# Products of ones in front of fifteen waits of TensorE, written into the work bank that is taken next

## The reference

```
x = x + xattn0(layernorm(x), ctx, mask, ...)    # 16 heads of 32, masked softmax
x = x + ffn0(layernorm(x), packed ternary weight, scale, bias)
x = x + xattn1(layernorm(x), ctx, ...)          # 16 heads of 64, softmax, Wo
x = x + ffn1(layernorm(x), w_freq, bias)        # fft, product, inverse fft
```

## Time and profile before

| | |
|---|---|
| three runs, median (lowest to highest) | 1057.13 us (1056.42 to 1057.41) |
| the profiled execution | 1054.12 us |
| its span in the profile | 1052.3 us |
| mean granted clock of TensorE over the span | 0.952 |
| PE busy | 904.6 us (86%), 6236 matmuls |
| DVE busy | 837.3 us (80%) |
| ACT busy | 639.2 us (61%) |
| POOL busy | 576.9 us (55%) |

### The profile page before, as it was taken

The page is one execution under the profiler, slowest core; times in us unless marked ns, Lnnn a source line. Parts: engine busy times, 40 slices in busy tenths (PEclk is TensorE's granted clock), DMA queues, the critical chain, the costliest instruction groups (busy, mean ns, idle before and its releaser), DMA issues. The chain is left out here.

```text
span 1052.3 us, 17974 instructions
## 1 busy us (share of the span) xinstructions
PE 904.6 (86%) x6236; PEld 498.7 (47%) x6236; DVE 837.3 (80%) x1451; ACT 639.2 (61%) x1792; POOL 576.9 (55%) x596
## 2 busy tenths in 40 slices
PE   0698988696888989998999899989999998798598
PEld 0446764252544554544455445545554545344343
DVE  7777968489999789979978997898889978755624
ACT  2435755275786487758765976697568756615610
POOL 2404774535274569456954784677378554636303
PEclk9999989798898999999999999999999999899599
DMA  9570475857574766765694669385946655621605
GB/s 290 133 173 20 102 147 131 166 119 206 95 124 96 132 113 125 151 137 108 119 190 92 119 114 201 66 152 105 204 78 128 120 91 117 109 64 36 125 1 160
DMA packets 352906, 130.41 MB, mean 124 GB/s; under 512 B 333487, under 2 KB 342640, under 8 KB 349999
## 3 DMA queue, kind: packets, MB, share of 16 engines
q1 hardware_dynamic: 352815, 129.25, 60.1%
HBM read 33.57 MB, written 15.96 MB: 47 GB/s over the span
## 5 line engine op out<-in xcount | busy, mean ns | idle before, releaser
L878 POOL TENSOR_TENSOR pr<-pr,sm 128x616 f32<-128x616 f32 x128 | 177.5, 1387 | 230.0 <-DVE sm L1391 230.0
L1031 ACT ACTIVATE pr<-scores,bound,factor 128x77 f32<-128x77 f32 x576 | 230.1, 418 | 6.9 <-ACT bound L1025 0.4
L262 PE MATMUL wb<-xT,wq_hl 128*128 128x512 f16 (+1 forms) x400 | 152.1, 380 | 14.7 <-DMA xT<-xh 7.7
L263 PE MATMUL wb<-xT,wq_hl 128*128 128x512 f16 (+1 forms) x400 | 151.8, 379 | 0.0
L264 PE MATMUL wb<-xT,wq_hl 128*128 128x512 f16 (+1 forms) x400 | 151.6, 379 | 0.0
L1031 ACT ACTIVATION_READ_ACCUMULATOR pr<-scores,bound,factor 128x1 f32 x576 | 119.3, 207 | 0.0
L1044 ACT ACTIVATE ph<-pr 128x618 f16<-128x618 f32 x128 | 93.3, 729 | 41.2 <-POOL pr L878 33.4
L262 PE MATMUL wb<-wo_hl,qc 128*128 128x512 f16 x276 | 106.0, 384 | 8.3 <-DVE wo_hl L1166 6.7
L263 PE MATMUL wb<-wo_hl,qc 128*128 128x512 f16 x276 | 105.7, 383 | 0.0
L264 PE MATMUL wb<-wo_hl,qc 128*128 128x512 f16 x276 | 105.6, 383 | 0.0
L1396 DVE SCALAR_TENSOR_TENSOR ph<-pr,ph 128x618 f16<-128x618 f32 x80 | 89.2, 1115 | 10.5 <-ACT ph L1044 10.2
(11 more groups left out here) (232 smaller groups left out, 2452.1 us busy)
## 6 DMA issues: line engine op xcount, KB each, us to landing
xr<-in_x SPq DMA_DIRECT2D x6, 1024.0 KB, 6.4
out_x<-xr SPq DMA_DIRECT2D x5, 1024.0 KB, 5.5
xr<-in_wk SPq DMA_DIRECT2D x3, 1024.0 KB, 7.1
xr<-in_wq SPq DMA_DIRECT2D x3, 1024.0 KB, 10.2
xr<-in_wv SPq DMA_DIRECT2D x3, 1024.0 KB, 5.7
k1b<-scr_k SPq DMA_DIRECT2D x16, 154.0 KB, 4.3
scr_k<-k1b SPq DMA_DIRECT2D x7, 308.0 KB, 7.3
x<-in_x SPq DMA_DIRECT2D x2, 1024.0 KB, 7.2
```

The costliest lines, as they stand in the source:

```text
L262: pe.matmul(out, lhs(0), rhs(0), start=start, stop=False, **kw)
L263: pe.matmul(out, lhs(0), rhs(1), start=False, stop=False, **kw)
L878: pool.tensor_tensor(v, v, s, ALU.mult).then_inc(probs_ready, 1)
L1031: ins = act.activation(pr[U % 3][:, h // 4, cols], sc[:, U % 2, h // 4, cols], ACT.Exp, bias=bound[:, U % 2, h:h + 1], scale=k["factor"][: ...
```

## The change

Before 15 of TensorE's waits it issues a number of matmuls, ones times ones, 128x128 by 128x512 in bfloat16, into the bank of the next fill. Nobody reads them: the fill that takes the bank begins with start=True. In front of them stands the wait for that bank (`bank_free`), also where a score unit follows that takes no bank. The keys of `WARM` name the fill or unit before which they stand; the numbers are the counts, 184 in all.

```diff
+WARM = {("S", "v0", 0, 0): 11, ("X", "pv", 2, 0): 19, ("S", "v1", 0, 0): 19, ("Y", "q", 0, 0): 20, ("Y", 0, 0): 19,
+        ("W", "q", 0, 2): 6, ("X", 2, 2): 12, ("Y", "pv", 4, 0): 6, ("Y", 6, 6): 10, ("Z", "f", 2, 5): 15,
+        ("Y", 4, 7): 8, ("Y", 5, 7): 7, ("Y", 6, 7): 6, ("Y", "pv", 0, 7): 8, ("Y", "pv", 4, 7): 18}
...
+NEXT_FILL = [sum(len(v) for v in SLOT_FILLS[:g]) for g in range(len(SLOTS))]
...
+            def in_step(use, n):
+
+                if n >= WB:
+                    pe.wait_ge(bank_free, n - WB + 1)
+                for _ in range(WARM[use]):
+                    pe.matmul(wb[:, n % WB, :].rearrange("p (c n) -> p c n", c=4), ones[:, :],
+                              ones[:, :].rearrange("p (c n) -> p c n", c=1).broadcast_to([P, 4, P]), start=True, stop=True)
+
             pe.wait_ge(zeroed, 1)
             for g, (i, s) in enumerate(SLOTS):
                 follows = unit_at(g + 1)
                 if follows and follows[:2] != ("Y", 0):
+                    if follows in WARM:
+                        in_step(follows, NEXT_FILL[g])
                     scores(*follows)
                 for use in SLOT_FILLS[g]:
+                    if use in WARM:
+                        in_step(use, FILL[use])
                     fill(use)
                 if follows and follows[:2] == ("Y", 0):
+                    if follows in WARM:
+                        in_step(follows, NEXT_FILL[g + 1])
                     scores(*follows)
```

## The result

The changed kernel takes 1059.54 us (median of 14 runs, 1057.50 to 1062.77), the kernel before in the same session 1056.68 us (14 runs, 1054.65 to 1059.11). The ratio is 1.0029, with a 95% interval of 1.0017 to 1.0042: 3.1 us slower, by 1.8 to 4.4. That is more than the 0.2% that a measurement can tell. The time lies inside the predicted range, 1052.0 to 1062.7 us; the forecast, +1.0 us and no change that can be told, was 2 us too low. The profiled execution took 1057.59 us, 3.5 more than the one of before.

The account below looks back on a forecast made before the run. The prediction saw gains only at the program's two ends, where TensorE's waits halve its clock, often beside other engines' bounds. Terms +5.2 early, -2.3 and -1.9 late sum to +1.0 on the 1057.13 median: 1058.1 us, range 1052.0 to 1062.7.

Parts of the forecast that it names:

- The exposed bursts: Bursts at ("S","v0",0,0) and ("X","pv",2,0) start only once their late bank is free, delaying real work: +2.3 and +3.8 us.
- The first term: At ("S","v0",0,0), 11 products run 4.6 us at half clock after the wait; half is given back: +2.3 us.
- Early sum: Places before about 335 us: 2.3 + 3.8 + 0.2 - 1.1 = +5.2 us, passed on whole by the repeating steps.
- ("X",2,2): +0.2: Late bank near 312 us: 12 products end 0.9 us after the wait; full-clock scores give back nearly all.
- The rival's half-clock burst of 5.0 us: At ("X",2,2), the clock falls before the burst, so 12 products take 5.0 us: +2.5 instead of +0.2.
- term of -1.1 at ("Y","pv",4,0): From 321.72 us, 36 products at full clock; VectorE's idling goes and the split-weights wait at 331.67 ends sooner: -1.1 us.
- The late gains: Full clock after 908.40 us at ("Z","f",2,5), -2.3 us, and for the last 36 products at ("Y","pv",4,7), -1.9 us.
- the places before the exponentials: Four places ("Y",4,7) to ("Y","pv",0,7), 957 to 997 us, where ScalarE's exponentials and transpositions are the chain: 0.
- Rival 1: Leftover idling drops the clock before 908.40 us (+3.3, 1060.4), at ("X",2,2), or both (1062.7); chance 0.30.
- Rival 2: VectorE's other work hides the exposed bursts before 188 us: 1054.3, or 1052.0 if both go; chance 0.20.
- Rival 4: Products of ones don't count as work, so the clock falls as before and bursts run late: 1073; chance 0.05.
- Rival 3: Half clock costs half its duration wherever it is low, TensorE being the bound there: -33 us, 1024; chance 0.03.

Follow-up runs that it names:

- e2: The kernel before plus only the bursts at ("S","v0",0,0) and ("X","pv",2,0), 11 and 19 products behind their late banks: 1061.79 us, ratio 1.0049.
- e1: The changed kernel without the bursts at ("S","v0",0,0) and ("X","pv",2,0), the other 13 kept: 1054.10 us, ratio 0.9972 to the kernel before.
- e11: The kernel before plus only the bursts at ("S","v0",0,0) and ("X","pv",2,0), written into free scores places: 1054.16 us, ratio 0.9983.
- e3: The kernel before plus only the late bursts at ("Z","f",2,5) and ("Y","pv",4,7), 15 and 18 products: 1053.17 us, ratio 0.9973.
- e8: The kernel before plus only the six covered bursts from 183 to 325 us: 1055.22 us, ratio 0.9985.
- e9: The changed kernel with all 15 bank waits but no products: 1056.59 us, ratio 1.0001 to the kernel before.
- e7: The kernel before plus only the burst of 11 products at ("S","v0",0,0), behind the late bank: 1060.24 us, ratio 1.0034.
- e4: The changed kernel with the bursts at ("S","v0",0,0) and ("X","pv",2,0) written into free scores places: 1050.43 us, ratio 0.9944 to the kernel before.
- e5: e4 plus six products before ("Z","out",0,0), the wait for split weights: 1048.27 us, ratio 0.9938 to the kernel before.
- e6: e5 plus 4 products before ("Y",4,b) for b from 1 to 5 and 3 for b = 6: 1049.17 us, ratio 0.9939 to the kernel before.
- e12: e5 plus four products before each of five middle waits for the transposed input xT: 1051.71 us, ratio 0.9951 to the kernel before.
- e10: e5 plus 9 products before ("S","s",5,0) and 24 before ("X",2,1): 1047.94 us, ratio 0.9916 to the kernel before.

## Why the prediction was right, and where it failed

**The exposed bursts: right in sum.** Said +2.3 and +3.8. e2 measures +5.2 us, and e1 beside the change 6 us. The mechanism is as it was told: the rows of the ones begin at 50.42 and 139.03 behind the wait for the bank, at half clock, and VectorE's wait of 2.56 us moved 4.9 us later without shrinking. e11 shows it from the other side: with a free place to write, the same two bursts cost nothing. The first term looks too large in the time line (about 1.3). The burst ran for 3.86 us, not 4.6, since the clock came back at 53.1 and not at 56.3; the Trainium skill, page "TensorE: Matmul & The Clock Gate", section "What's actually happening", says that the point at which the clock changes differs from run to run. The traces agree: the two points lie 3.2 us apart, and e3, e8 and e9, which have no burst here, were at half clock for some 3.4 us (e3 at 0.50 from 51.9 to 55.1), not for 6.7 as in the earlier trace rows. So the prediction worked out its term from one trace that was at half clock longer here than the others. But e7's median has +3.6, so no number is put on it alone.

**Early sum: right up to 331 us.** Said: TensorE's row at 331.67 lies about 5 us later. It stands at 336.14, 4.5 us later, with a longer wait. The rows at 188.39 and 199.32 were to move by 6 us and moved by 4.9. ScalarE's wait is unchanged, 15.16 us for 15.14: faster values before 188 us gave nothing, as said.

**("X",2,2): +0.2, right as far as can be seen.** The 12 products took 2.76 us, full clock, behind a wait of 1.77 us. The rival's half-clock burst of 5.0 us did not come.

**The step that failed: "From there on TensorE is dense, and I take it that the repeating steps pass a shift on whole", with its term of -1.1 at ("Y","pv",4,0).** The time saved there is real and has the size that was told: VectorE's four reads stand in one row without idling (331.19; 0.32 and 0.79 us before), and its shift falls by 1.3 between 323 and 329 us, from +5.7 to +4.4. But it is given back at once. TensorE comes sooner to a wait that VectorE's split weights end, the wait grows from 1.51 to 2.36 us, the clock falls behind it for 3.4 us, and the shift is +6.0 at 338. The prediction named a leftover wait as the danger, but at 908 us, and said of the middle that it had nothing to give; it had something to lose. The same fall stands in e1 and e4, and e5's six products take it away. In place of the -1.1 the runs show +0.3: 1.3 us gained, 1.6 us lost. The other +1.5 of the changed kernel, between 338 and 420 us, arises at full clock, 1.3 of it where ScalarE waits 1.43 us for a late transposition of the probabilities and VectorE 0.61 us for ScalarE (rows at 399.41 and 400.17). The kernel before has no wait there. Why the transfer is late is open; e6 and e12 have the same step near 790 us, so it isn't shown that the change brings it. The two losses, 1.6 and 1.5 us, are 3.1 us of a single execution, where the forecast was 2 us too low in the median. That the fall explains the miss is therefore what the traces show, not the medians, in which e5 can't be told from e4.

**The late gains: right.** Said -2.3 and -1.9. In the changed kernel TensorE's shift goes from +7.6 at 908.40 to +5.6 at 971.32, and VectorE's from +5.6 to +3.7 by 1026. Between them, to 994.5 us, the shift stays at +5.6, although the clock is now up there for all but 3.4 us: the places before the exponentials gave 0, as said. The stretch from 906 to 923 us has clock 1.00, and the last 36 products take 4.08 us (said 4). e3's -2.9 us, by itself, is a little less than the -3.9 of its own trace. The last gain isn't there in every execution: in the traces of e1 and e10 the wait behind the 18 products was 2.91 and 4.11 us instead of 2.3, the clock was down behind it, and the gain was 0.3 us in the one and a loss of 1.9 us in the other.

**Rival 1** (the clock falls before 908): the place held. The leftover wait was 1.58 us, not 2.7, and the clock behind it was 1.00. What it said in general, that a leftover wait lets the clock fall, is what happened, 570 us sooner, and in e1 and e10 at the last products, too. The result, slower by more than 0.2%, is this rival's side.

**Rival 2** is refuted by e2. **Rival 4** (ones don't hold the clock) is refuted by the clock of 0.985. **Rival 3**: the mean clock rose by 0.033, and a mean of 0.985 leaves 2 x 0.015 x 1056 = 32 us at half clock where 0.952 left 101. By the rule of the Trainium skill (page "TensorE: Matmul & The Clock Gate", section "Terms"), the 69 us that went would be worth, as an estimate, 35 us. Even e5, with 0.988 and no exposed burst, gained 6.5, so here the rule doesn't hold. e8 is the plainest case: its clock of 0.969 means some 35 us less at half clock, and it gained 1.6 us. Such stretches lie where TensorE isn't what the others wait for.

**The 131 ns** that the Trainium skill gives for a matmul of N=512 (same page, section "Back-to-back issue gap") do not appear here either: 18 products of ones in a row took 4.06 us, 0.22 us each, as the prediction took it from before.

## What to carry to other kernels

Work that is only there to keep a clock up must be able to start when the wait starts: look at what the burst itself waits for, and give it a place to write that nobody holds (the same 184 products: +0.3% with 30 of them behind a late bank, -0.6% with the 30 in a free place). Then follow the time that is gained to the next wait on that engine, since it makes that wait longer. And weigh throttled time by who is the bound behind it: here 76 us less of it (e5, where a clock of 0.988 leaves 2 x 0.012 x 1043 = 25 of 101 us) were worth 6.5 us by the ratio (3.4 to 9.8), once nothing was exposed.

## What the runs showed that was not expected

Time that is saved in front of a wait can bring the clock down behind it: where 1.51 us of waiting before the split weights were harmless, 2.36 us were followed by 3.4 us at half clock. The length of the wait alone doesn't settle it, as waits of 2.74 us in e6 and 2.68 us in e9 left the clock at 1.00, and those of 2.75 (e4), 2.72 (e1) and 2.81 us (e10) brought it down. That a fall in a dense stretch costs half of what it lasts (1.6 us for 3.4 us), where the 20 us at half clock beside ScalarE's exponentials cost nothing (the shift is +5.6 at 949.8 and still at 994.5 us, with the clock up for all but 3.4 us of the stretch), is the same clock at two prices.

A transposing transfer arrives late in single repetitions, at no fixed place. For `xT` it is some 1.7 us, at 385, 386, 388, 594, 693 and 789 us in six traces (e6, e12, e4, e9, e1, e10); for `prT` it shows in ScalarE's waits of 1.4 to 1.5 us in the changed kernel, e6 and e12. No run here shows why.

Executions of one kernel differ by more than the change is worth: from 4 us between the fastest and the slowest run (e3, e8) to 14 (e5). The kernels with a mean clock of 0.98 and more spread no less than the kernel before, and in them the slower executions have the lower clock. Steps of 1 to 2 us at full clock, such as those in e6, e7, e12 and the changed kernel, are part of it, and the largest step of each of these four comes behind a wait for a transposition of the probabilities. A kernel like this wants a dozen runs of each side before a term of 2 us can be seen.
